# The last convolution of a graph network: edge rows loaded two steps ahead, a ring of eight, and another order of PE's and ACT's work in a step

## The chip, the cores and the metric

The kernel runs on one core of a Trainium2 chip. The metric is the device time of one execution in microseconds (us), lower is better. The median of three runs of the kernel before is 12377.51 us.

## The reference

Four message-passing layers of a graph network run one after the other on 6250 nodes and 100000 edges; after each, `x = layernorm(x + layer(x))`. The change touches the edge part of the last layer alone. Cut to that part:

```python
h = silu(edge_scalars @ fcW1 * (1.0 / sqrt(8)))          # (E, 8) @ (8, 64)
w = h @ fcW2 * (1.0 / sqrt(64))                          # (E, 64) @ (64, 192)
wA, wB, wC, wD = w[:, :64], w[:, 64:128], w[:, 128:160], w[:, 160:192]
xs, xv = f_s[edge_src], f_v[edge_src]                    # gather: 64 scalars, 32 vectors of 3
y0, y1 = edge_attr[:, :1], edge_attr[:, 1:4]
outA = wA * xs * y0
outD = wD * einsum('eud,ed->eu', xv, y1) / sqrt(3)
outB = wB[:, :, None] * xs[:, :, None] * y1[:, None, :]
outC = wC[:, :, None] * xv * y0[:, :, None]
edge_feat = concatenate([outA, outD, outB, outC])        # 384 numbers an edge
agg = segment_sum(edge_feat, edge_dst, num_segments=n)   # edges are sorted by edge_dst
```

All of it is float32. `tab_src` in the kernel holds f_s and f_v of each node (160 numbers).

## The kernel before, in words

`plain_convolution` (lines 1718 to 1881) does this part. Edges are taken in macro tiles of 4 x 128 (TM = 4 edges on each of 128 partitions). The loop has V = 244 entries, which the text below calls edge steps or indices: 196 macro tiles and 48 more passes over tiles that straddle a block of target nodes. A table `W["block"]` says which tile an index reads.

For an index i the work runs in stages on five queues, each stage one or more steps after the one before it. An engine's program is a list of steps; in step n it does, in the order in which the code has them, each of its stages for index n minus the stage's number (TURN 0, PRE 1, WEIGHTS 2, PRODUCT 3, SUM 4, TOTAL 5, STORE 6). The engines are held together only by semaphores.

- SP loads the edge rows `er` (128 x 64 floats, line 1751) and stores `total` (line 1755). The load for index i waits until `products` of index i - 4 are done, because `er` has four buffers. Its block number comes from memory by a `value_load`.
- POOL waits for `er`, issues 4 indirect DMAs that gather 128 node rows each into `g` (line 1772), and adds a shift to the target numbers, `rel` (line 1775). `g` and `rel` also have four buffers.
- PE (TensorE) turns the edge rows (TURN, `psE`, line 1789), multiplies them by the first map (PRE, `psH`, line 1803), the result by the second (WEIGHTS, `psW`, line 1810), and sums the products by a one-hot matrix (SUM, `psS`, line 1796). In the profile one float32 matmul is two records.
- ACT copies the turned rows (`esT`, line 1822), applies silu (`h`, line 1827), and scales the gathered rows (`feat_y`, `g0` in the code, four instructions, line 1833).
- DVE makes the products in `rows` (lines 1853 to 1868, the last one signals `products`), the one-hot matrix `hot` (line 1870), and adds `psS` to a running `total` (line 1877).

`steps` writes the first and last steps out and loops over the rest, RING steps to a turn of the loop. `psE` and `psH` have one buffer; `psW`, `psS`, `rows`, `hot`, `esT`, `h` and `g0` have two.

Of the kernel before, what the change touches and what calls it, by code (L numbers as in the profile page):

```python
# [16 lines left out]
I32 = mybir.dt.int32  # L17
ALU = mybir.AluOpType
ACT = mybir.ActivationFunctionType
AX = mybir.AxisListType  # L20

P = 128
N_NODES, N_EDGES = 6250, 100000
C0, C1 = 64, 32
C1V = 3 * C1
CX = C0 + C1V
# [5 lines left out]
TM = 4  # L32
# [6 lines left out]
V = NM + BOUNDS  # L39
ER = 16  # L40
# [4 lines left out]
class Names:  # L45
# [17 lines left out]
    def sem(self, name):  # L63
        if name not in self.sems:
            self.sems[name] = self.nc.alloc_semaphore(f"{self.tag}_{name}")
        return self.sems[name]


def wait(eng, sem, value):

    if not isinstance(value, int) or value > 0:
        eng.wait_ge(sem, value)


def wait_apart(eng, sem, value, passed):

    if not isinstance(value, int):
        eng.wait_ge(sem, value)
        eng.sem_inc(passed, 1)
    elif value > 0:  # L80
        eng.wait_ge(sem, value)
# [41 lines left out]
def bcast(ap, axis, n):  # L123

    ap = ap.unsqueeze(axis)
    shape = list(ap.shape)
    shape[axis] = n
    return ap.to_broadcast(shape)
# [456 lines left out]
def comp(ap, n=3):  # L585

    return ap.rearrange("p t (d c) -> p t d c", d=n)
# [1130 lines left out]
def plain_convolution(nc, W, D, tag):  # L1718

    TURN, PRE, WEIGHTS, PRODUCT, SUM, TOTAL, STORE = 0, 1, 2, 3, 4, 5, 6
    LAST, RING = STORE, 4
    width = SUM_W[3]
    sums = D["sums"][3]
    with ExitStack() as ctx:
        S = Names(nc, ctx, tag)
        sem = S.sem
        ring = lambda name, shape, n, dt=F32: [S.sb(f"{name}{u}", shape, dt) for u in range(n)]
        er, g = ring("er", [P, TM, ER], RING), ring("g", [P, TM, CX], RING)  # L1730
        rel, hot = ring("rel", [P, TM], RING, I32), ring("hot", [P, TM, P], 2)
        esT, h = ring("esT", [ER * TM, P], 2), ring("h", [64, ME], 2)
        g0, prod, dot, bs = ring("feat_y0", [P, TM, CX], 2), S.sb("prod", [P, TM, C1V]), S.sb("dot", [P, TM, C1]), S.sb("bs", [P, TM, C0])
        rows, total = ring("rows", [P, TM, width], 2), ring("total", [P, width], RING)
        psE, psH = S.ps("psE", [ER * TM, 512]), S.ps("psH", [64, 512])
        psWs = [S.ps(f"psW{u}", [P, TM, 256]) for u in range(2)]
        psS = [S.ps(f"psS{u}", [P, 512]) for u in range(2)]
# [3 lines left out]
        @block.sync  # L1741
        def _(sp):
            sp.dma_start(sums[0], W["zeros"][:, 0:width]).then_inc(sem("first"), 16)

            def body(i_of):
                if m := i_of(0):
                    i, u, j = m
                    wait_apart(sp, sem("products"), i - RING + 1, sem("sp_passed"))
                    wait_apart(sp, sem("rel"), i - RING + 1, sem("sp_passed"))
                    at = sp.value_load(W["block"][0:1, bass.ds(i, 1)], min_val=0, max_val=NM - 1)  # L1750
                    sp.dma_start(er[u][:, :, :].rearrange("p t c -> p (t c)"), block_at(edges, at)).then_inc(sem(f"er{u}"), 16)
                if m := i_of(STORE):
                    i, u, j = m
                    wait_apart(sp, sem("totals"), i + 1, sem("sp_passed"))
                    sp.dma_start(sums[bass.ds(i + 1, 1), :, :].rearrange("o p c -> (o p) c"), total[u][:, :]).then_inc(sem(f"stored{u}"), 16)

            steps(sp, V, LAST, body, RING)
            sp.wait_ge(sem("first"), 16)
            for u in range(RING):
                sp.wait_ge(sem(f"stored{u}"), 16 * (V // RING))  # L1760

        @block.gpsimd
        def _(pool):
            passed = sem("pool_passed")

            def body(i_of):
                if m := i_of(0):
                    i, u, j = m
                    wait_apart(pool, sem(f"er{u}"), (j + 1) * 16, passed)
                    wait_apart(pool, sem("products"), i - RING + 1, passed)  # L1770
                    for k in range(TM):
                        pool.indirect_dma_start(g[u][:, k, :], None, D["tab_src"], bass.IndirectOffsetOnAxis(er[u][:, k, 12:13].bitcast(I32), 0))\  # L1772
                            .then_inc(sem(f"gathered{u}"), 16)
                    wait_apart(pool, sem("hot"), i - RING + 1, passed)
                    nc.gpsimd.tensor_tensor(rel[u][:, :], er[u][:, :, 13].bitcast(I32), W["shift"][:, bass.ds(i, 1)].to_broadcast([P, TM]), ALU.add)\
                        .then_inc(sem("rel"), 1)

            steps(pool, V, LAST, body, RING)

        @block.tensor  # L1780
        def _(pe):
            passed = sem("pe_passed")

            def body(i_of):
                if m := i_of(TURN):
                    i, u, j = m
                    wait_apart(pe, sem(f"er{u}"), (j + 1) * 16, passed)
                    wait_apart(pe, sem("esT"), i, passed)
                    nc.tensor.transpose(psE[:, 0:P], er[u][:, :, :].rearrange("p t c -> p (t c)"), W["ident"][:, :]).then_inc(sem("es_T"), 1)
                if m := i_of(SUM):  # L1790
                    i, u, j = m
                    wait_apart(pe, sem("hot"), i + 1, passed)
                    wait_apart(pe, sem("products"), i + 1, passed)
                    wait_apart(pe, sem("totals"), i - 1, passed)
                    for k in range(TM):
                        last = nc.tensor.matmul(psS[u % 2][:, 0:width], hot[u % 2][:, k, :], rows[u % 2][:, k, :], start=(k == 0), stop=(k == TM - 1))  # L1796
                    last.then_inc(sem("summed"), 1)
                if m := i_of(PRE):
                    i, u, j = m
                    wait_apart(pe, sem("esT"), i + 1, passed)  # L1800
                    wait_apart(pe, sem("h"), i, passed)
                    for k in range(TM):
                        last = nc.tensor.matmul(psH[:, P * k:P * k + P], W["l3_fc1"][:, 64 * k:64 * k + 64], esT[u % 2][:, :], start=True, stop=True)
                    last.then_inc(sem("pre"), 1)
                if m := i_of(WEIGHTS):
                    i, u, j = m
                    wait_apart(pe, sem("h"), i + 1, passed)
                    wait_apart(pe, sem("products"), i - 1, passed)
                    for k in range(TM):
                        last = nc.tensor.matmul(psWs[u % 2][:, k, 0:192], h[u % 2][:, P * k:P * k + P], W["l3_fc2"][:, :], start=True, stop=True)  # L1810
                    last.then_inc(sem("weights"), 1)

            steps(pe, V, LAST, body, RING)

        @block.scalar
        def _(act):
            def body(i_of):
                if m := i_of(TURN):
                    i, u, j = m
                    act.wait_ge(sem("es_T"), i + 1)  # L1820
                    wait(act, sem("pre"), i - 1)
                    nc.scalar.activation(esT[u % 2][:, :], psE[:, 0:P], ACT.Copy).then_inc(sem("esT"), 1)
                if m := i_of(PRE):
                    i, u, j = m
                    act.wait_ge(sem("pre"), i + 1)
                    wait(act, sem("weights"), i - 1)
                    nc.scalar.activation(h[u % 2][:, :], psH[:, :], ACT.Silu, scale=1.0 / float(np.sqrt(8.0))).then_inc(sem("h"), 1)
                if m := i_of(WEIGHTS):
                    i, u, j = m
                    act.wait_ge(sem(f"gathered{u}"), (j + 1) * 16 * TM)  # L1830
                    wait(act, sem("products"), i - 1)
                    for k in range(TM):
                        last = nc.scalar.activation(g0[u % 2][:, k, :], g[u][:, k, :], ACT.Copy, scale=er[u][:, k, 8:9])
                    last.then_inc(sem("g0"), 1)

            steps(act, V, LAST, body, RING)

        @block.vector
        def _(dve):
            tt = nc.vector.tensor_tensor  # L1840
            nc.vector.memset(total[RING - 1][:, :], 0.0).then_inc(sem("empty"), 1)

            def body(i_of):
                if m := i_of(PRODUCT):
                    i, u, j = m
                    psW, R = psWs[u % 2], rows[u % 2]
                    s, v = g[u][:, :, 0:C0], comp(g[u][:, :, C0:CX])
                    s0, v0 = g0[u % 2][:, :, 0:C0], comp(g0[u % 2][:, :, C0:CX])
                    D3 = R[:, :, 96:width].rearrange("p t (d c) -> p t d c", d=3)
                    Y = bcast(er[u][:, :, 9:12], 3, C1)  # L1850
# [16 lines left out]
                    dve.wait_ge(sem("dot"), i + 1)  # L1867
                    tt(R[:, :, C0:96], psW[:, :, 160:192], dot[:, :, :], ALU.mult).then_inc(sem("products"), 1)
                    dve.wait_ge(sem("rel"), i + 1)
                    tt(hot[u % 2][:, :, :], bcast(W["lane"][:, :], 1, TM), bcast(rel[u][:, :], 2, P), ALU.is_equal).then_inc(sem("hot"), 1)  # L1870
                if m := i_of(TOTAL):
                    i, u, j = m
                    dve.wait_ge(sem("summed"), i + 1)
# [935 lines left out]
```

## Time and profile before

| | |
|---|---|
| median of 3 runs | 12377.51 us |
| lowest and highest run | 12340.81 and 12393.03 us |
| span of the profiled execution | 13633.7 us |
| this part, first to last start of its SUM matmuls | 11404.8 to 13286.7 us |

No time of the profiled execution other than its span is at hand. The span is 10% above the median of the runs, so a difference of durations in the trace is one of the profiled execution.

The page divides the span in 40 slices; this part lies in the slices 34 to 39. The views used below are the waits (who waited for whom), the groups of instructions, the timeline (instructions in order of time, with the idle time before each and who ended it), and the busy time of each engine in stretches, with the granted clock of TensorE as a share of full speed (1.00 is 2.4 GHz, 0.50 is 1.2 GHz).

### The profile page before, as it was taken

Reading aid. Unit: us, or ns where it says so; the run is one execution under the profiler, and the core shown is the slowest. Engines: PE = TensorE matmul, PEld = TensorE weight load, DVE = VectorE, ACT = ScalarE, POOL = GpSimd, SP = SyncE. Lnnn points to the kernel's source line nnn. Section 1 sums busy time; section 2 is a strip of 40 time slices with the busy share of each in tenths; the row PEclk is TensorE's granted clock in tenths of the full one; section 3 lists DMA queues with packets and bytes.
Section 4 is the critical chain, followed back from the end, with each engine's and each line's share of the span. In section 5 each row is a group of like instructions: output and inputs, shape, how many; then the busy total and the mean of one; then the engine's idle time right before and its main releaser. Section 6 shows DMA issues by size and latency. Waiting matters only on the chain. (4 is left out here: it accounts for less than half of the span.)

```text
span 13633.7 us, 220854 instructions
## 1 busy us (share of the span) xinstructions
PE 9563.9 (70%) x44805; PEld 7451.6 (55%) x44805; DVE 8593.3 (63%) x21214; ACT 4334.4 (32%) x10856; POOL 8081.0 (59%) x8212
## 2 busy tenths in 40 slices
PE   2998989863656666666655777777775657888885
PEld 2888888853544222222244666666664545555554
DVE  4677777778734555555534777777777765555553
ACT  1444444430022222222212555555554002222221
POOL 4777777755624888888822555555552643555550
PEclk7777777777956777777765888888887987888885
DMA  3444444435602888888852222222221652222221
GB/s 93 105 107 103 107 102 107 105 100 158 188 20 50 132 132 132 131 132 131 132 148 85 68 69 68 68 69 69 68 69 49 183 134 57 71 71 70 73 72 46
DMA packets 1350634, 1320.06 MB, mean 97 GB/s; under 512 B 508622, under 2 KB 1147330, under 8 KB 1349894
## 3 DMA queue, kind: packets, MB, share of 16 engines
q0 software_dynamic: 347904, 594.12, 23.6%
q1 hardware_dynamic: 854716, 713.61, 18.2%
q10 hardware_dynamic: 147914, 11.21, 0.8%
q8 instruction: 37, 0.61, 0.0%
q14 instruction: 63, 0.52, 0.0%
HBM read 800.64 MB, written 517.55 MB: 97 GB/s over the span
## 5 line engine op out<-in xcount | busy, mean ns | idle before, releaser
L737 POOL DMA_INDIRECT e_gs<-tab_src,e_ix x1568 | 1685.9, 1075 | 1253.8 <-DVE e_msg L2066 785.5
L737 POOL DMA_INDIRECT e_gd<-tab_dst,e_ix x1568 | 1670.5, 1065 | 478.0 <-issue 473.4
L676 PE MATMUL e_psF<-w_ident,e_F 128*128 128x128 f32 x6272 | 1394.2, 335 | 727.6 <-ACT e_F L1954 495.6
L788 PE MATMUL e_psS<-e_rows,e_same 128*128 128x480 f32 x1568 | 1113.4, 876 | 857.7 <-DVE e_same L762 857.7
L1772 POOL DMA_INDIRECT e_g<-tab_src,e_er x976 | 977.0, 1001 | 852.0 <-DMA e_er<-edge_rows 600.8
L676 PEld LDWEIGHTS e_psF<-w_ident,e_F 128*128 128x128 f32 x6272 | 951.5, 180 | 895.9 <-issue 844.5
L806 POOL DMA_INDIRECT acc<-e_sums,e_row x784 | 1248.6, 1593 | 239.0 <-issue 220.5
L706 ACT ACTIVATE e_FT<-e_psF 128x384 f32<-128x384 f32 (+1 forms) x2352 | 1069.7, 455 | 941.7 <-PE e_psF L676 587.3
L788 PEld LDWEIGHTS e_psS<-e_rows,e_same 128*128 128x128 f32 x1568 | 431.4, 293 | 1549.4 <-issue 1522.2
L1563 PE MATMUL s_psS<-s_wv,s_hot 128*128 128x168 f32 (+1 forms) x3904 | 714.2, 331 | 596.0 <-POOL s_wv L1521 574.8
L712 ACT ACTIVATE e_O<-e_psO 128x352 f32<-128x352 f32 (+1 forms) x1568 | 689.7, 440 | 995.6 <-remote 434.0
L1563 PEld LDWEIGHTS s_psS<-s_wv,s_hot 128*128 128x128 f32 x3904 | 606.7, 203 | 703.1 <-issue 490.4
L737 POOL DMA_INDIRECT e_g<-tab_src,e_ix x784 | 822.8, 1050 | 248.6 <-issue 183.2
L796 ACT ACTIVATE e_sums<-e_psS 128x480 f32<-128x480 f32 x784 | 447.8, 571 | 1513.7 <-issue 1089.8
L1796 PE MATMUL e_psS<-e_rows,e_hot 128*128 128x384 f32 x1952 | 914.7, 626 | 20.1 <-issue 14.6
L2266 POOL TENSOR_TENSOR n_st<-n_st,w_half 128x8 f32<-128x8 f32 x70 | 113.5, 1638 | 1085.4 <-DVE n_st L2691 937.1
L1684 DVE TENSOR_TENSOR e_prod<-e_g,e_dirs 128x384 f32<-128x384 f32 x196 | 109.4, 558 | 887.8 <-DMA e_g<-tab_src,e_ix 837.4
L1796 PEld LDWEIGHTS e_psS<-e_rows,e_hot 128*128 128x128 f32 x1952 | 459.1, 247 | 345.3 <-issue 230.2
L1485 POOL TENSOR_TENSOR s_wv<-s_val,s_pb 128x128 f32<-128x128 f32 x976 | 614.5, 649 | 0.0
L1855 DVE TENSOR_TENSOR e_bs<-e_psW,e_g 128x256 f32<-128x256 f32 x244 | 102.8, 421 | 785.5 <-remote 457.2
L686 PE MATMUL e_psO<-w_l_t,e_FT 128*128 128x160 f32 x1568 | 471.9, 394 | 98.2 <-ACT e_O L712 85.7
L2384 ACT ACTIVATE n_sT<-n_psA 64x512 f32<-64x512 f32 x70 | 41.4, 591 | 1441.0 <-PE n_psA L2280 1439.4
(492 smaller groups left out, 25450.2 us busy)
## 6 DMA issues: line engine op xcount, KB each, us to landing
s_val<-val SPq DMA_DIRECT2D x488, 320.0 KB
val<-e_O SPq DMA_DIRECT2D x392, 320.0 KB
acc<-w_zeros SPq DMA_DIRECT2D x392, 139.5 KB
n_ag<-acc SPq DMA_DIRECT2D x56, 960.0 KB
e_krow<-in_src_t SPq DMA_DIRECT2D x196, 256.0 KB
sums<-e_total SPq DMA_DIRECT2D x244, 192.0 KB
e_es<-in_es SPq DMA_DIRECT2D x196, 130.0 KB
e_gs<-tab_src,e_ix POOLq DMA_INDIRECT x1568
```

Of the source, the lines that this page charges most:

```text
L676: last = nc.tensor.transpose(psF[:, P * g:P * g + P], F[:, k, P * g:P * g + P], ident[:, :])
L686: nc.tensor.matmul(o[:, 0:first], f[:, 0:P], W[w + "_t0"][:, :], start=True, stop=True, skip_group_check=True)
L706: nc.scalar.activation(FT[:, k, :], psF[:, 0:width], ACT.Copy).then_inc(S.sem(tag + "_FT"), 1)
L712: nc.scalar.activation(O[:, k, :], o[:, 0:width], ACT.Copy).then_inc(S.sem(tag + "_O"), 1)
L737: pool.indirect_dma_start(into[t][u][:, k, :], None, tables[t], bass.IndirectOffsetOnAxis(ix[u][:, t, k:k + 1], 0))\
L788: nc.tensor.matmul(psS[(k) % len(psS)], T["same"][u][:, k, :], values[:, k, :], start=True, stop=True)\
L796: nc.scalar.activation(T["sums"][u][:, k, :], psS[k % len(psS)], ACT.Copy).then_inc(S.sem("sums"), 1)
L806: pool.indirect_dma_start(acc[k], bass.IndirectOffsetOnAxis(T["row"][u][:, k:k + 1], 0), T["sums"][u][:, k, :], None, compute_op=ALU.add). ...
L1485: return tt(heads(wv), heads(val), bcast(pb[u][:, :, :], 3, n // H), ALU.mult)
L1563: last = nc.tensor.matmul(psS[u][:, 0:width], hot[u][:, k, :], wv[u][:, k, :], start=(k == 0), stop=(k == TM - 1))
L1772: pool.indirect_dma_start(g[u][:, k, :], None, D["tab_src"], bass.IndirectOffsetOnAxis(er[u][:, k, 12:13].bitcast(I32), 0))\
L1796: last = nc.tensor.matmul(psS[u % 2][:, 0:width], hot[u % 2][:, k, :], rows[u % 2][:, k, :], start=(k == 0), stop=(k == TM - 1))
```

## The change

The stages get other numbers: the load of `er` stays at 0, gather, `rel` and TURN move from 0 to 2, and all others move by 2 as well. So seen from the gather, the load comes two steps earlier and nothing else moves by a whole step. `er`, `total` and their semaphores get eight buffers; `g` and `rel` keep four (ROWS4). The load for index i now waits for `products` of index i - 8. A turn of the loop holds eight steps in place of four.

Inside a step PE does TURN, PRE, WEIGHTS, SUM in place of TURN, SUM, PRE, WEIGHTS. ACT does `feat_y`, `esT`, `h` in place of `esT`, `h`, `feat_y`.

```diff
-    TURN, PRE, WEIGHTS, PRODUCT, SUM, TOTAL, STORE = 0, 1, 2, 3, 4, 5, 6
-    LAST, RING = STORE, 4
+    GATHER, PRE, WEIGHTS, PRODUCT, SUM, TOTAL, STORE = 2, 3, 4, 5, 6, 7, 8
+    TURN, LAST, RING, ROWS4 = GATHER, STORE, 8, 4
...
-        er, g = ring("er", [P, TM, ER], RING), ring("g", [P, TM, CX], RING)
-        rel, hot = ring("rel", [P, TM], RING, I32), ring("hot", [P, TM, P], 2)
+        er, g = ring("er", [P, TM, ER], RING), ring("g", [P, TM, CX], ROWS4)
+        rel, hot = ring("rel", [P, TM], ROWS4, I32), ring("hot", [P, TM, P], 2)
...
-                if m := i_of(0):
+                if m := i_of(GATHER):
                     i, u, j = m
                     wait_apart(pool, sem(f"er{u}"), (j + 1) * 16, passed)
-                    wait_apart(pool, sem("products"), i - RING + 1, passed)
+                    wait_apart(pool, sem("products"), i - ROWS4 + 1, passed)
...
-                    wait_apart(pool, sem("hot"), i - RING + 1, passed)
+                    wait_apart(pool, sem("hot"), i - ROWS4 + 1, passed)
...
@@ PE: the blocks PRE and WEIGHTS now stand ahead of SUM
+                if m := i_of(PRE):
...
+                if m := i_of(WEIGHTS):
...
                 if m := i_of(SUM):
...
-                if m := i_of(PRE):
...
-                if m := i_of(WEIGHTS):
...
@@ ACT: the block WEIGHTS (feat_y) now stands ahead of TURN and PRE
+                if m := i_of(WEIGHTS):
...
                 if m := i_of(TURN):
...
-                if m := i_of(WEIGHTS):
...
```

On PE, at the head of the loop of this part, one step before reads as follows (`L78` and `L106` are registers and the loop).

```order
L106 ISA
L78 REGISTER_ALU
L1789 MATMUL e_psE<-w_ident,e_er 64x128
L78 ISA
L78 REGISTER_ALU
L1796 MATMUL e_psS<-e_rows,e_hot 128x384 x4
L78 REGISTER_ALU x2
L1803 MATMUL e_psH<-e_esT,w_l_fc 64x128 x4
L1810 MATMUL e_psW<-w_l_fc,e_h 128x192 x4
```

The same place of the changed kernel, where PRE has line 1795, WEIGHTS 1802 and SUM 1810:

```order
L106 ISA
L78 ISA
L1789 MATMUL e_psE<-w_ident,e_er 64x128
L78 REGISTER_ALU
L1795 MATMUL e_psH<-e_esT,w_l_fc 64x128 x4
L78 REGISTER_ALU
L1802 MATMUL e_psW<-w_l_fc,e_h 128x192 x4
L78 REGISTER_ALU
L1810 MATMUL e_psS<-e_rows,e_hot 128x384 x4
```

The sum of 4 matmuls has moved behind the two maps; no matmul was added or taken away.

On ACT, in the second step of the loop, the order before was:

```order
L1822 ACTIVATE e_esT<-e_psE 64x128
L1827 ACTIVATE e_h<-e_psH 64x512
L1833 ACTIVATE e_feat_y<-e_g,e_er 128x160 x4
```

And now, with `feat_y` at line 1823, `esT` at 1829 and `h` at 1834:

```order
L1823 ACTIVATE e_feat_y<-e_g,e_er 128x160 x4
L1827 REGISTER_ALU
L1829 ACTIVATE e_esT<-e_psE 64x128
L1834 ACTIVATE e_h<-e_psH 64x512
```

The four scalings of gathered rows now stand first, so whatever they wait for holds the copy of the turned rows too.

## Rows read from the trace of the kernel before

**Rows 1.** Windows: busy us (count) of each engine, granted clock, DMA share.

```profile
core 0: us, PE busy (x) PEld busy (x) DVE busy (x) ACT busy (x) POOL busy (x), PEclk, DMA share, GB/s
11400.00:13290.00 1890.00, 1579.99 (x6072) 992.68 (x6071) 1081.43 (x2438) 514.94 (x1455) 1031.26 (x1212) 0.83 0.27 72
```

**Rows 2.** Waits, 11420 to 13250 us: who waited for whom, total us, times, longest.

```profile
POOL e_g L1772 <- DMA e_er<-edge_rows: 577.6, 135, 9.2
...
DVE e_bs L1855 <- remote: 449.4, 61, 11.7
...
PE e_psE L1789 <- DMA e_er<-edge_rows: 274.7, 118, 5.2
```

**Rows 3.** Timeline of PE: start, us, what, idle time before it.

```profile
12302.54 0.30 PE L1789 MATMUL e_psE<-w_ident,e_er 128*64 128x128 f32 x1
12302.68 2.75 PE L1796 MATMUL e_psS<-e_rows,e_hot 128*128 128x384 f32 x8
12305.35 1.08 PE L1803 MATMUL e_psH<-e_esT,w_l_fc 64*64 64x128 f32 x8
12306.37 1.56 PE L1810 MATMUL e_psW<-w_l_fc,e_h 64*128 64x192 f32 x8
12309.95 0.39 PE L1789 MATMUL e_psE<-w_ident,e_er 128*64 128x128 f32 x1 [2.02 <-DMA e_er<-edge_rows]
12310.41 5.46 PE L1796 MATMUL e_psS<-e_rows,e_hot 128*128 128x384 f32 x8
...
12318.31 0.30 PE L1789 MATMUL e_psE<-w_ident,e_er 128*64 128x128 f32 x1
```

**Rows 4.** Timeline of DVE, SP's queue and POOL: the load behind that wait.

```profile
12305.85 0.28 DVE L1868 TENSOR_TENSOR e_rows<-e_psW,e_dot 128x128 f32<-128x128 f32 x1
...
12307.73 0.34 SPq L1751 DMA_DIRECT2D e_er<-edge_rows  x1
...
12310.47 0.97 POOL L1772 DMA_INDIRECT e_g<-tab_src,e_er  x1 [3.70 <-DMA e_er<-edge_rows]
```

**Rows 5.** Windows around that wait.

```profile
12308.00:12309.00 1.00, 0.00 (x0) 0.00 (x0) 0.89 (x2) 1.00 (x4) 0.00 (x0) 0.98 0.14 31
...
12310.00:12312.00 2.00, 1.94 (x4) 1.07 (x5) 2.00 (x6) 0.27 (x1) 1.22 (x2) 0.50 0.00 0
```

**Rows 6.** Timeline of POOL: one step that waited for no load.

```profile
12301.14 0.20 POOL L1775 TENSOR_TENSOR e_rel<-e_er,w_shift 128x4 int32<-128x4 int32 x1
12301.50 0.97 POOL L1772 DMA_INDIRECT e_g<-tab_src,e_er  x1 [0.15 <-issue]
...
12304.02 0.95 POOL L1772 DMA_INDIRECT e_g<-tab_src,e_er  x1 [0.30 <-issue]
...
12306.29 0.48 POOL L1775 TENSOR_TENSOR e_rel<-e_er,w_shift 128x4 int32<-128x4 int32 x1
```

**Rows 7.** Sources: count, ns min/median/max of one, first and last start.

```profile
L1772 POOL DMA_INDIRECT e_g<-tab_src,e_er x976: 942/949/1542, 11390.7 to 13267.4; - x196
...
L1866 DVE TENSOR_TENSOR e_rows<-e_bs,e_er x488: 539/547/615, 11401.1 to 13282.6; 128x384 f32<-128x384 f32 x163
...
L1796 PE MATMUL e_psS<-e_rows,e_hot x1952: 486/486/980, 11404.9 to 13287.0; 128*128 128x384 f32 x196
```

**Rows 8.** Groups and a window of the first layer: its gathers, its engines' load.

```profile
L737 POOL DMA_INDIRECT e_gs<-tab_src,e_ix x1568 | 1685.9, 1075 | 1253.8 <-DVE e_msg L2066 785.5
500.00:2400.00 1900.00, 1703.19 (x9368) 1564.84 (x9366) 1372.42 (x3412) 870.34 (x1842) 1461.24 (x1288) 0.75 0.43 106
```

**Rows 9.** Timeline of DVE: one index, to the next `prod`.

```profile
12319.11 0.42 DVE L1855 TENSOR_TENSOR e_bs<-e_psW,e_g 128x256 f32<-128x256 f32 x1 [5.78 <-PE e_psW L1810]
...
12319.95 0.41 DVE L1861 TENSOR_TENSOR e_rows<-e_psW,e_feat_y 128x256 f32<-128x256 f32 x1
...
12321.88 0.68 DVE L1870 TENSOR_TENSOR e_hot<-w_lane,e_rel 128x512 f32<-128x512 int32 x1
...
12323.00 0.55 DVE L1853 TENSOR_TENSOR e_prod<-e_g,e_er 128x384 f32<-128x384 f32 x1
```

More of the change, by code:

```diff
@@ L1759, in _ @@
             for u in range(RING):
-                sp.wait_ge(sem(f"stored{u}"), 16 * (V // RING))
+                sp.wait_ge(sem(f"stored{u}"), 16 * -(-(V - u) // RING))
         @block.gpsimd
@@ L1766, in body @@
             def body(i_of):
-                if m := i_of(0):
+                if m := i_of(GATHER):
                     i, u, j = m
                     wait_apart(pool, sem(f"er{u}"), (j + 1) * 16, passed)
-                    wait_apart(pool, sem("products"), i - RING + 1, passed)
+                    wait_apart(pool, sem("products"), i - ROWS4 + 1, passed)
                     for k in range(TM):
-                        pool.indirect_dma_start(g[u][:, k, :], None, D["tab_src"], bass.IndirectOffsetOnAxis(er[u][:, k, 12:13].bitcast(I32), 0))\
+                        pool.indirect_dma_start(g[u % ROWS4][:, k, :], None, D["tab_src"], bass.IndirectOffsetOnAxis(er[u][:, k, 12:13].bitcast(I32), 0))\
                             .then_inc(sem(f"gathered{u}"), 16)
-                    wait_apart(pool, sem("hot"), i - RING + 1, passed)
-                    nc.gpsimd.tensor_tensor(rel[u][:, :], er[u][:, :, 13].bitcast(I32), W["shift"][:, bass.ds(i, 1)].to_broadcast([P, TM]), ALU.add)\
+                    wait_apart(pool, sem("hot"), i - ROWS4 + 1, passed)
+                    nc.gpsimd.tensor_tensor(rel[u % ROWS4][:, :], er[u][:, :, 13].bitcast(I32), W["shift"][:, bass.ds(i, 1)].to_broadcast([P, TM]), ALU.add)\
                         .then_inc(sem("rel"), 1)
@@ L1789, in body @@
                     nc.tensor.transpose(psE[:, 0:P], er[u][:, :, :].rearrange("p t c -> p (t c)"), W["ident"][:, :]).then_inc(sem("es_T"), 1)
[L1790 to L1797, printed above, removed]
                 if m := i_of(PRE):
@@ L1811, in body @@
                     last.then_inc(sem("weights"), 1)
+                if m := i_of(SUM):
+                    i, u, j = m
+                    wait_apart(pe, sem("hot"), i + 1, passed)
+                    wait_apart(pe, sem("products"), i + 1, passed)
+                    wait_apart(pe, sem("totals"), i - 1, passed)
+                    for k in range(TM):
+                        last = nc.tensor.matmul(psS[u % 2][:, 0:width], hot[u % 2][:, k, :], rows[u % 2][:, k, :], start=(k == 0), stop=(k == TM - 1))
+                    last.then_inc(sem("summed"), 1)
             steps(pe, V, LAST, body, RING)
@@ L1817, in body @@
             def body(i_of):
+                if m := i_of(WEIGHTS):
+                    i, u, j = m
+                    act.wait_ge(sem(f"gathered{u}"), (j + 1) * 16 * TM)
+                    wait(act, sem("products"), i - 1)
+                    for k in range(TM):
+                        last = nc.scalar.activation(g0[u % 2][:, k, :], g[u % ROWS4][:, k, :], ACT.Copy, scale=er[u][:, k, 8:9])
+                    last.then_inc(sem("g0"), 1)
                 if m := i_of(TURN):
@@ L1827, in body @@
                     nc.scalar.activation(h[u % 2][:, :], psH[:, :], ACT.Silu, scale=1.0 / float(np.sqrt(8.0))).then_inc(sem("h"), 1)
-                if m := i_of(WEIGHTS):
[L1829 to L1834, printed above, removed]
             steps(act, V, LAST, body, RING)
@@ L1846, in body @@
                     psW, R = psWs[u % 2], rows[u % 2]
-                    s, v = g[u][:, :, 0:C0], comp(g[u][:, :, C0:CX])
+                    s, v = g[u % ROWS4][:, :, 0:C0], comp(g[u % ROWS4][:, :, C0:CX])
                     s0, v0 = g0[u % 2][:, :, 0:C0], comp(g0[u % 2][:, :, C0:CX])
@@ L1869, in body @@
                     dve.wait_ge(sem("rel"), i + 1)
-                    tt(hot[u % 2][:, :, :], bcast(W["lane"][:, :], 1, TM), bcast(rel[u][:, :], 2, P), ALU.is_equal).then_inc(sem("hot"), 1)
+                    tt(hot[u % 2][:, :, :], bcast(W["lane"][:, :], 1, TM), bcast(rel[u % ROWS4][:, :], 2, P), ALU.is_equal).then_inc(sem("hot"), 1)
                 if m := i_of(TOTAL):
```

## The prediction

> **What bounds the kernel now.** The kernel is a chain of parts, so only the last convolution counts. Its SUM matmuls start from 11404.9 to 13287.0 us [rows 7]; for 244 indices that is 243 intervals, 1882.1 us, 7.745 us each. The windows show no engine full: PE 84% (1579.99 of 1890 us), DVE 57%, POOL 55%, DMA 27%, at a granted clock of 0.83 [rows 1]. So something waits in rings, and the waits say for what: POOL waited 577.6 us and PE 274.7 us for one thing, the load of the edge rows [rows 2]. Two thirds of DVE's waits (449.4 us) have no releaser on record; its product waits for weights that PE makes, so I count them as PE's lateness.
>
> The timeline of PE shows the rhythm, in pairs. An undisturbed step is SUM, PRE, WEIGHTS and a turn: from 12302.54 to 12307.93, less an overlap of 0.06 as there is between PRE and WEIGHTS: 5.33 us, PE's floor. Then PE stands 2.02 us for the load, and its next SUM takes 5.46 us in place of 2.75; two steps took 12318.31 - 12302.54 = 15.77 us [rows 3]. Why the load is late: the last product of an index ends at 12306.13, SP issues the load 1.6 us later at 12307.73, and gather and turn can start at 12310.47 and 12309.95, 3.8 us after the product at best [rows 4]. The load waits for the product four indices back, and the turn that needs it is first in PE's step: the ring is one load too short. The slow SUM is the clock: it was still 0.98 in the first us of the idle time, and it was 0.50 from 12310 on, although PE was busy again [rows 5]. PE's idle time is thus paid twice.
>
> The interval splits as 5.33 (floor) + 1.16 (274.7 us over the 236 steps of that stretch [rows 2]) + 1.26 left, which I put down to the half clock: 2.71 us more for one SUM in each pair would be 1.35.
>
> **The change, part by part.** All terms are us of an interval, in the profiled execution.
>
> *The load, two steps ahead, eight buffers.* It is issued after the product eight indices back. The gather of index m may not start before products of m - 4 (`g` still has four buffers), and the load of m needs only those of m - 8, which is four intervals, over 20 us, earlier; SP does it behind a store that waits for a total of an older index. Against 3.8 us of latency this leaves slack of many us. Removed: 1.16 on PE, and POOL's 577.6 us of waits. With PE no longer idle, the 1.26 of half clock should go as well. Lower bound if only these count: 5.33. If this cover failed (SP kept back by its store), the old 3.8 us would be back in every step.
>
> *PE's order.* The same matmuls. PRE now follows TURN, but reads the copy made one step earlier; WEIGHTS reads silu of the step before, and one whole SUM (2.75 us) lies between. New: PE's last work of a step is SUM, and DVE writes `rows` over those that SUM two indices back has read. DVE can start with `bs` and `dot` after WEIGHTS, but must then wait for SUM's end, that is for the end of PE's step. From the first write of `rows` to the end of `hot` it needs 12322.56 - 12319.95 = 2.61 us; the whole index, from `bs` to the end of the next `prod`, takes 12323.55 - 12319.11 = 4.44 [rows 9]. The next SUM that needs these rows comes a full PE step and two maps later, about 8 us. Cost 0; hidden by PE's own step. Behind DVE's wait stand `hot` and `total`, for which PE waits only one step later, so the same slack covers them.
>
> *ACT's order.* `feat_y` needs gathers two steps old and products of m - 4, which end about 3 us before the step in which its copy is wanted; ACT's own work is 514.94 us over 244 indices, 2.1 us [rows 1]. Cost 0; without that cover a late gather would hold `esT`, and through it PE's next turn.
>
> *Longer loop.* Eight steps a turn, 28 turns for 58, two steps more to fill and drain in which only a load or a store runs: under 2 us together, not counted.
>
> *What is late next.* DVE needs 4.44, PE 5.33. POOL: an unhindered step is 12306.29 - 12301.14 = 5.15 us: `rel`, 0.15, and four gathers of 0.95 to 0.97 with 0.30 between them [rows 6]. That is nearly PE's floor, and it will not stay unhindered: gathers here take 949 ns in the median and up to 1542 [rows 7]. So far POOL had its busy times when DVE often stood still. The nearest row with a denser DVE is the first layer's: DVE 1372.42 of 1900 us, 72%, gathers of 1075 ns in the mean [rows 8]. DVE will be about 80% busy (4.44 of 5.6). Four gathers of 1.075, three gaps of 0.30, `rel` at 0.25 (0.20 and 0.48 in rows 6) and 0.15 behind it make 5.60. Bounds: 5.15 from below, and from above all gathers and `rel` at the longest seen, 4 x 1.542 + 0.90 + 0.48 + 0.15 = 7.70. I take 5.60, since the first layer's mean is the nearest row; POOL then sets the pace, not PE, and PE idles 0.27 us a step, too little by rows 5 to think that the clock falls.
>
> **A rule weighed.** DVE's products of two operands in SBUF (line 1866) took 539 to 615 ns, whatever POOL did [rows 7]; gathers, on the other hand, went up to 1542. The Trainium skill, "SBUF — State Buffer", section "SBUF: two separate sides", says that a DVE instruction with two SBUF inputs and a GpSimd one that reads SBUF exclude each other for their whole length. By this rule no gather would run beside lines 1853, 1866 or 1870. The trace agrees by half: the gather pays, DVE never does by more than 0.07 us. What full exclusion would give is a rival below.
>
> **The sum.** 7.745 - 5.60 = 2.145 us, times 243 is 521 us of the span of 13633.7. The runs' median is 9.2% under that span, and nothing shows which waits shrink without the profiler. If all shrink alike, the gain is 521 x 0.908 = 473; if this part doesn't shrink, 521. The middle is 497, a factor of 0.954: 12377.5 - 497 = 11880 us.
>
> **Rivals.**
> 1. *The part is worth less unprofiled* (0.18). If the interval before shrinks by 9.2% to 7.03 while matmul and gather times stay, the gain is 1.43 x 243 = 347: 12030 us. If the load's latency shrinks more than the mean, less still, to about 12150. For it: load latency and SP's 1.6 us are waits, the stuff that a profiler stretches. Against: half of the loss sits in matmuls at half clock.
> 2. *POOL and DVE exclude each other* (0.10). Then a step of POOL is its busy time, 4 x 0.949 + 0.208, plus DVE's `prod`, two of line 1866 and `hot`, 0.55 + 1.09 + 0.68 [rows 7, 9]: 6.32 us; gain 1.42 x 243 x 0.954 = 330: 12047 us. For it: the maxima of the gathers. Against: in rows 6 the gather at 12304.02 took 0.95 with DVE at work.
> 3. *No change* (0.06): another ring takes over the wait at once, at about 7.7 us. The candidate is `g` with four buffers: gather (5.15), landing (taken as the load's 2.2 us, 12309.95 less 12307.73), `feat_y` and product (about 2 and 4.4) around four indices, 13.8 / 4 = 3.4 us a step. It does not reach 5.33, so I give it little.
> 4. *Slower* (0.05): the clock stays at half though PE works. A PE step is then twice the floor, 10.66 us, and the gain turns into a loss of 2.915 x 243 x 0.954 = 676 us: 13053. It decides from the point where 45% of the steps run so, (7.745 - 5.33) / 5.33. For it: in the first layer PE is 90% busy and the granted clock is 0.75 [rows 8]; with half of the time at half clock the step would be 5.33 / 0.75 = 7.11, still faster, at 12230. Against: rows 3 and 5, where a fully busy PE brought the clock back within one step.
> 5. *Better than my case* (0.03): POOL at 5.15 and PE at 5.33, unshrunk, 2.415 x 243 = 587: 11790 us.
>
> **How the numbers follow.** My forecast, an interval of 5.3 to 5.9, has 0.58. It covers about 11790 to 12000. A measurement of this kernel tells about 0.5% from no change (62 us). The range runs from 11790, case 5, to 12100, which takes in rival 2 and most of rival 1: 0.58 + 0.10 + 0.13, about 0.8. Faster by over 0.5% are the forecast and rivals 1, 2 and 5, 0.89, less a little for the smallest of rival 1: 0.88. Within 0.5%: 0.07. Slower: 0.05.
>
> **What would show it.** In the changed kernel's profile: the waits of PE and POOL for `er` gone; SUM matmuls 1360 us from first to last; granted clock above 0.95 in the part; POOL nearly without waits, gathers near 1075 ns; DVE waiting for `summed` each step, less than 1 us. Wrong would be: PE waiting for ACT's copy at its turn (a late gather), a clock near 0.8 with SUM matmuls of 980 ns, gathers above 1.2 us in the mean, or the interval after falling in the trace and not in the runs.

## The result and the profile after

| | before | changed |
|---|---|---|
| median of 4 timed runs, us | 12382.14 | 12152.06 |
| lowest and highest run, us | 12340.81, 12393.03 | 12142.17, 12165.48 |
| this part, first to last SUM, profiled | 1882.1 [rows 7] | 1309.8 |
| one interval (243 of them), profiled | 7.745 | 5.39 |

The ratio is 0.983, 95% interval 0.9814 to 0.9847. The change makes the kernel faster, by 230 us, less than half of the 497 forecast; the time lies above the range. The traces show a larger difference, 572 us in this part alone, but the two profiled executions are not alike: that of the kernel before has a span of 13633.7 us, 10% above its timed runs, that of the changed kernel 12140.4, and that execution took 12142.17 us. What the first trace shows is told under the experiments.

The changed kernel's windows over all of this part and inside it (columns as in [rows 1]):

```profile
10480.00:11800.00 1320.00, 1315.61 (x6060) 891.36 (x6059) 1081.99 (x2431) 542.63 (x1452) 1040.84 (x1208) 1.00 0.38 102
10600.00:11700.00 1100.00, 1100.00 (x5097) 746.12 (x5096) 907.54 (x2040) 457.81 (x1224) 879.14 (x1021) 1.00 0.39 103
```

From 10600 to 11700 us PE is busy all the time, at full granted clock. Its waits from 10600 to 11700 us, and the sources that answer to [rows 7]:

```profile
ACT e_esT L1829 <- PE e_psE L1789: 296.4, 204, 1.6
ACT e_feat_y L1823 <- DMA e_g<-tab_src,e_er: 196.4, 204, 1.1
DVE e_rows L1861 <- PE e_psS L1810: 192.5, 204, 0.9
POOL e_g L1772 <- issue: 188.7, 626, 0.3
```

```profile
L1810 PE MATMUL e_psS<-e_rows,e_hot x1952: 486/486/1007, 10486.2 to 11796.0; 128*128 128x384 f32 x196
...
L1772 POOL DMA_INDIRECT e_g<-tab_src,e_er x976: 942/946/1121, 10467.1 to 11780.8; - x196
```

No engine waits for `er` in this stretch, against 577.6 and 274.7 us in [rows 2]. ACT waits in each step for the gathered rows (196.4 us in 204 waits), which costs nothing here, because PE doesn't wait for ACT. The timeline, PE and one instruction of DVE, shows a step of 5.39 us without a hole, from turn to turn:

```profile
11200.54 2.85 PE L1810 MATMUL e_psS<-e_rows,e_hot 128*128 128x384 f32 x8
11203.23 0.27 PE L1789 MATMUL e_psE<-w_ident,e_er 128*64 128x128 f32 x1
11203.43 0.42 DVE L1861 TENSOR_TENSOR e_rows<-e_psW,e_feat_y 128x256 f32<-128x256 f32 x1 [0.94 <-PE e_psS L1810]
11203.43 1.08 PE L1795 MATMUL e_psH<-e_esT,w_l_fc 64*64 64x128 f32 x8
11204.44 1.56 PE L1802 MATMUL e_psW<-w_l_fc,e_h 64*128 64x192 f32 x8
...
11208.62 0.27 PE L1789 MATMUL e_psE<-w_ident,e_er 128*64 128x128 f32 x1
```

DVE now waits 0.94 us for the end of SUM before it may write `rows`, as forecast.

### The profile page after: what moved, and what is told of

The parts are those of the page before. It is cut to its first block and busy times, and to the rows that moved or that the text cites. A ratio compares the mean times of both kernels' runs of the same rounds, so it can differ in the third digit from the quotient of the medians.

```text
span 12140.4 us, 219938 instructions
## 1 busy us (share of the span) xinstructions
PE 8894.9 (73%) x44805; PEld 7005.1 (58%) x44805; DVE 8560.0 (71%) x21214; ACT 4341.0 (36%) x10856; POOL 8069.6 (66%) x8212
## 5 line engine op out<-in xcount | busy, mean ns | idle before, releaser
L737 POOL DMA_INDIRECT e_gd<-tab_dst,e_ix x1568 | 1732.2, 1105 | 477.8 <-issue 477.5
L737 POOL DMA_INDIRECT e_gs<-tab_src,e_ix x1568 | 1640.0, 1046 | 501.3 <-issue 436.3
L676 PE MATMUL e_psF<-w_ident,e_F 128*128 128x128 f32 x6272 | 1264.6, 310 | 245.3 <-ACT e_F L1954 232.7
L676 PEld LDWEIGHTS e_psF<-w_ident,e_F 128*128 128x128 f32 x6272 | 876.1, 166 | 377.6 <-issue 336.4
L1810 PE MATMUL e_psS<-e_rows,e_hot 128*128 128x384 f32 x1952 | 696.7, 500 | 0.8 <-DVE e_total L1877 0.8
L1010 DVE TENSOR_TENSOR e_hn<-e_raw,e_rstd 128x256 f32<-128x256 f32 x398 | 151.4, 422 | 509.5 <-POOL e_rstd L884 509.5
L1810 PEld LDWEIGHTS e_psS<-e_rows,e_hot 128*128 128x128 f32 x1952 | 351.9, 190 | 251.3 <-issue 56.4
L983 PE MATMUL e_psW<-w_l_rw,e_h 65*128 65x224 f32 x1568 | 393.5, 401 | 139.4 <-DVE e_F L1072 134.6
```

Of the source, the lines that this page charges most:

```text
L676: last = nc.tensor.transpose(psF[:, P * g:P * g + P], F[:, k, P * g:P * g + P], ident[:, :])
L737: pool.indirect_dma_start(into[t][u][:, k, :], None, tables[t], bass.IndirectOffsetOnAxis(ix[u][:, t, k:k + 1], 0))\
L983: last = nc.tensor.matmul(psW[:, k, 0:224], h2[v][:, P * k:P * k + P], W["l0_rw3"][:, :], start=True, stop=True)
```

## The experiments

Two questions: why the gain was 230 us and not 497, and which part of the change makes it. On the first, theory A says that the trace shown before had more waits than the timed runs; its rival says that the interval really was 7.7 us and that the gain was lost elsewhere. On the second, the forecast had put everything on the loads and nothing on the order. All times are medians; "before" is the kernel before on the same chip. The chips differ: the kernel before takes about 12350 us on some, called ordinary below, and about 14060 on others, called slow chips, so only times of one chip are compared.

### The kernel before again, and this part twice

The first run is the kernel before, unchanged. The second calls this part a second time, with buffers of its own and the same output:

```diff
                 plain_convolution(nc, W, D, "e3")
+                plain_convolution(nc, W, D, "f3")
```

> The kernel before, unchanged, profiled once more. Theory A (the trace of before was taken in a slow execution, and the runs that are timed are faster in this part too): the span comes out near the timed 12382 us, not 13634, and the SUM matmuls of the last convolution take about 1540 us from first to last, 6.3 us an interval, since the change left 1310 us and gained 230; POOL's and PE's waits for the edge rows are well under the 577.6 and 274.7 us shown. Rival B (the profiler stretches this kernel each time, and not the changed one): the span is again near 13630 us and the interval near 7.7 us, while the time measured stays at 12382.

> The kernel before with its last convolution run twice in a row, which leaves the output as it is. The added time is what the part costs without any help of a profile. Theory A: 1540 us more than before, about 13920 us in all. Rival B': the part does cost 1880 us in timed runs, and the change loses 340 us elsewhere: 1880 us more, about 14260.

Measured: 12348.27 us, ratio 1.0003 (0.9988 to 1.0018), and 13905.45 against 12350.51, ratio 1.1262 (1.1221 to 1.1304), so a second call costs 1555 us. Theory A had forecast 1540, its rival 1880. Sources, waits (10700 to 11800 us) and window of the kernel before, again:

```profile
L1796 PE MATMUL e_psS<-e_rows,e_hot x1952: 486/486/980, 10472.6 to 11983.8; 128*128 128x384 f32 x196
```

```profile
DVE e_bs L1855 <- PE e_psW L1810: 297.1, 176, 4.1
...
POOL e_g L1772 <- DMA e_er<-edge_rows: 119.5, 74, 3.0
...
PE e_psE L1789 <- DMA e_er<-edge_rows: 41.6, 71, 0.9
```

```profile
10700.00:11800.00 1100.00, 1024.92 (x4487) 669.62 (x4486) 796.53 (x1791) 373.49 (x1074) 757.63 (x896) 0.97 0.34 91
```

The interval is 1511.2 / 243 = 6.22 us, and the added call takes 1555 unprofiled against 1882.1 in the first trace: theory A holds, its rival falls. PE waits for the same loads, but 0.23 us a step (41.6 us over 179.5 steps) in place of 1.16, and no wait is put down to "remote", the name that the view gives to a wait whose releaser it doesn't find. The span is 12331.6 and this execution took 12333.45 us, beside a median of 12348.27: here the profile did not stretch the execution.

The spans of this trace and of the changed kernel's differ by 191.2 us, their parts by 201.4: on ordinary executions trace and runs agree.

### Loads alone, order alone

Loads alone is the changed kernel with the blocks of PE and ACT back in their old order; order alone is the kernel before with the two orders of the changed one. Shown for PE:

```diff
@@ loads alone, against the changed kernel
+                if m := i_of(SUM):
...
                 if m := i_of(PRE):
...
-                if m := i_of(SUM):
...
@@ order alone, against the kernel before
-                if m := i_of(SUM):
...
                 if m := i_of(PRE):
...
+                if m := i_of(SUM):
...
```

> The changed kernel with PE's and ACT's order of before: loads two steps ahead, ring of eight. Theory A says that the loads are the whole change: 12152 us, as the changed kernel, interval 5.4 us, granted clock 1.00. Rival C (the order does part of it, since SUM then no longer stands between a turn and the first map): slower than the changed kernel by over 0.5%, 12215 us or more.

> The kernel before with PE's and ACT's new order alone; loads, stage numbers and rings as before. Theory A: within 0.5% of before, 12320 to 12445 us, the waits for edge rows unchanged. Rival C: over 0.5% faster than before. Third: slower than before by over 0.5%, since the turn that waits for the edge rows now holds both maps back directly, with no SUM between.

Measured, on the chip of the last two: loads alone 12120.42, ratio 0.9809 (0.9777 to 0.9841), interval (11773.4 - 10478.5) / 243 = 5.33; order alone 12143.77, ratio 0.9831 (0.98 to 0.9862), interval (11803.1 - 10481.1) / 243 = 5.44. The first came out as theory A has it, rival C fell: the new order is not needed for the gain. But the second was a miss for theory A: order alone, which the forecast held to be worth nothing, brings nearly as much as the whole change. Its sources and its window:

```profile
L1810 PE MATMUL e_psS<-e_rows,e_hot x1952: 485/486/1007, 10481.1 to 11803.1; 128*128 128x384 f32 x196
```

```profile
10600.00:11700.00 1100.00, 1093.33 (x5050) 739.30 (x5049) 898.80 (x2020) 452.30 (x1210) 880.04 (x1009) 1.00 0.39 102
```

### Which of the two orders

> The kernel before with PE's new order alone (SUM last in a step), rings and loads as before. Theory E (the order alone gained 207 us because DVE does its first two products during SUM, so that the last product, and with it the load of the edge rows, comes 0.9 us earlier after PE's last step): as the kernel with both orders, about 12145 us. Rival F (ACT's order did it: feat_y no longer stands behind silu): no gain, 12350.

> The kernel before with ACT's new order alone (feat_y first). Theory E: no gain, 12310 to 12400 us. Rival F: about 12145.

The edits are the halves of the last one, PE's blocks alone and ACT's alone. Measured against 12349.75: PE's order 12162.91, ratio 0.984 (0.9817 to 0.9862), interval (11807.1 - 10485.9) / 243 = 5.44; ACT's 12346.21, ratio 0.9987 (0.9974 to 0.9999), interval (12000.0 - 10475.6) / 243 = 6.27. All but 4 us of it is PE's order. One of the four runs with PE's order took 19345.35 us, the other three 12156.51 to 12165.2; why is not known, and without it the median would be 12160.62. The mechanism stands in the timelines, of DVE, SP's queue and PE. First the kernel before, again:

```profile
11202.93 1.56 PE L1810 MATMUL e_psW<-w_l_fc,e_h 64*128 64x192 f32 x8
...
11204.53 0.42 DVE L1855 TENSOR_TENSOR e_bs<-e_psW,e_g 128x256 f32<-128x256 f32 x1 [0.87 <-PE e_psW L1810]
...
11207.10 0.28 DVE L1868 TENSOR_TENSOR e_rows<-e_psW,e_dot 128x128 f32<-128x128 f32 x1
...
11208.35 0.34 SPq L1751 DMA_DIRECT2D e_er<-edge_rows  x1
...
11214.83 0.34 SPq L1751 DMA_DIRECT2D e_er<-edge_rows  x1
...
11216.91 0.27 PE L1789 MATMUL e_psE<-w_ident,e_er 128*64 128x128 f32 x1 [0.51 <-DMA e_er<-edge_rows]
```

PE's step ends with WEIGHTS, at 11204.49. DVE begins with `bs` 0.04 later and its last product ends at 11207.38; the load goes out 0.97 later, and 2.08 us after a load (11214.83 to 11216.91) a turn that waited for it can start. Together 0.04 + 2.85 + 0.97 + 2.08 = 5.94 us from the end of one step to the turn of the next but one, and between the two lies one step of 5.33: by this sum the turn waits 0.61, then the step after has no wait, and so in pairs. The waits shown by this trace at three turns in a row are 0.60, none and 0.51. Such a wait often costs more than itself:

```profile
10655.86 0.27 PE L1789 MATMUL e_psE<-w_ident,e_er 128*64 128x128 f32 x1 [0.55 <-DMA e_er<-edge_rows]
10656.52 4.51 PE L1796 MATMUL e_psS<-e_rows,e_hot 128*128 128x384 f32 x8 [0.39 <-issue]
```

Of the 206 SUMs from 10600 to 11900 us 31 took over 4 us. Now order alone:

```profile
11205.32 0.27 PE L1789 MATMUL e_psE<-w_ident,e_er 128*64 128x128 f32 x1
...
11205.52 0.42 DVE L1861 TENSOR_TENSOR e_rows<-e_psW,e_feat_y 128x256 f32<-128x256 f32 x1 [1.29 <-PE e_psS L1810]
...
11207.26 0.28 DVE L1868 TENSOR_TENSOR e_rows<-e_psW,e_dot 128x128 f32<-128x128 f32 x1
...
11208.50 0.33 SPq L1751 DMA_DIRECT2D e_er<-edge_rows  x1
...
11210.76 0.27 PE L1789 MATMUL e_psE<-w_ident,e_er 128*64 128x128 f32 x1
```

SUM is last here, from 11202.63 on, so DVE has done `bs` (from 11203.31) and `dot` (from 11203.64) under it and needs only the writes of `rows` after it. The load goes out 3.18 us after the next turn began, that is after the end of SUM; with 2.08 from load to turn that is 5.26, under PE's own 5.39. The wait goes because the loop got shorter, without another buffer.

### Load one step ahead

This is the changed kernel with eight buffers, gather one step behind the load:

```diff
-    GATHER, PRE, WEIGHTS, PRODUCT, SUM, TOTAL, STORE = 2, 3, 4, 5, 6, 7, 8
+    GATHER, PRE, WEIGHTS, PRODUCT, SUM, TOTAL, STORE = 1, 2, 3, 4, 5, 6, 7
```

> The changed kernel with the load one step ahead of the gather in place of two, ring of eight. The load then has one more interval, 5.4 us, against about 3.2 us of latency. Theory A: the same as the changed kernel, 12140 to 12165 us, no waits for edge rows. Rival (two steps are needed): waits for edge rows return, over 12200 us.

It was run with the changed kernel, loads alone and the changed kernel with this part called twice, on a chip where the kernel before takes 14068.76 us.

> The changed kernel once more, in five rounds, beside the version with early loads and the old order. Known so far: 12152 us, interval 5.39 us. Expected: 12140 to 12165.

> Early loads with the old order of PE and ACT, in five rounds on the same chip as the changed kernel. The trace of the first run had 5.33 us an interval against 5.39 with the new order, 15 us in all. Theory D (the new order costs a seam on PE, once the loads are early): 12115 to 12140 us, at least 10 us under the changed kernel. Rival: the two are equal, and the 12120 of the first run was the chip.

> The changed kernel with its last convolution run twice. Adds the part's cost with no profile: 1330 us (1310 for the SUM matmuls and 20 to fill and drain, as the kernel before twice added 1555 for 1540), so about 13480 us. The difference of the two doublings, 1555 less 1330, is then the gain of about 225 us. If the added time is above 1400, part of the gain is lost outside of the part.

Measured: one step ahead 13730.56, ratio 0.9757 (0.9724 to 0.9789); changed 13718.99, 0.9759 (0.9733 to 0.9786); loads alone 13738.92, 0.9765 (0.9738 to 0.9792); called twice 15420.62, 1.0969 (1.0933 to 1.1004), 1702 us over the changed kernel. One step ahead is as good as two on this chip; on an ordinary one it was not run. The expectations in absolute times were for an ordinary chip. That of loads alone, at least 10 us under the changed kernel, was missed: it was 20 us over. The limit of 1400 us for the second call can't be applied either, since the part takes 13369.2 - 11707.9 = 1661.3 us here, and the kernel before was not called twice on this chip. Here PE is not always busy in the changed kernel; its waits and its window from 11800 to 12800 us:

```profile
ACT e_esT L1829 <- remote: 320.3, 46, 8.9
...
POOL e_g L1772 <- DVE e_rows L1868: 213.6, 50, 5.3
...
DVE e_bs L1855 <- remote: 124.7, 25, 8.7
```

```profile
11800.00:12800.00 1000.00, 894.72 (x3635) 589.87 (x3634) 642.69 (x1453) 305.30 (x872) 630.87 (x725) 0.90 0.30 81
```

"remote" is back, and it is also in the trace on which the forecast rests [rows 2].

### A later load, before and after

SP reads the block number from memory three times in place of once ahead of each load, in the kernel before and in the changed one:

```diff
                     at = sp.value_load(W["block"][0:1, bass.ds(i, 1)], min_val=0, max_val=NM - 1)
+                    at = sp.value_load(W["block"][0:1, bass.ds(i, 1)], min_val=0, max_val=NM - 1)
+                    at = sp.value_load(W["block"][0:1, bass.ds(i, 1)], min_val=0, max_val=NM - 1)
```

> The kernel before with the block number read three times in place of once before each load of edge rows, which delays the load by an estimated 1.0 to 1.4 us (a whole product end to load issue takes 0.97 us with one read). Theory A (in the kernel before the load's latency lies on the chain product, load, turn, weights, product, once an interval): the whole delay is added to each interval, 240 to 340 us, to 12590 to 12690 us. Rival G (SP's work is hidden and the interval is set elsewhere): under 60 us more.

> The changed kernel with the same two further reads before each load. Theory A: nothing, since the load is issued over 15 us before it is needed, and SP has 5.39 us for about 4: within 0.5% of 12152. Rival: SP becomes the bound or holds the stores back, and over 60 us are added.

Measured: before with it 12650.02, ratio 1.0232 (1.0214 to 1.0251), interval (12303.1 - 10487.7) / 243 = 7.47; changed with it 12135.95, ratio 0.9822 (0.9804 to 0.984), interval 5.39. The kernel before got 300 us slower, within the 240 to 340 forecast, the changed one did not: its load has time to spare. Waits from 10700 to 12100 us, the window and the timeline of PE, DVE and SP's queue of the kernel before with the late load (lines are 2 further down):

```profile
POOL e_g L1774 <- DMA e_er<-edge_rows: 415.8, 97, 5.8
...
PE e_psE L1791 <- DMA e_er<-edge_rows: 167.1, 93, 2.1
```

```profile
10700.00:12100.00 1400.00, 1212.25 (x4657) 761.62 (x4656) 827.68 (x1860) 387.48 (x1118) 784.21 (x931) 0.84 0.27 74
```

```profile
11196.49 2.75 PE L1798 MATMUL e_psS<-e_rows,e_hot 128*128 128x384 f32 x8
...
11203.58 0.39 PE L1791 MATMUL e_psE<-w_ident,e_er 128*64 128x128 f32 x1 [1.84 <-DMA e_er<-edge_rows]
11204.24 5.46 PE L1798 MATMUL e_psS<-e_rows,e_hot 128*128 128x384 f32 x8 [0.27 <-issue]
...
11204.35 0.28 DVE L1870 TENSOR_TENSOR e_rows<-e_psW,e_dot 128x128 f32<-128x128 f32 x1
...
11206.71 0.34 SPq L1753 DMA_DIRECT2D e_er<-edge_rows  x1
```

This is the picture of [rows 3] on an ordinary chip: pairs, 1.84 us of idle time, a SUM of 5.46 (granted clock 0.50 from 11204 to 11210). A later load alone makes such waits, and the long matmuls come with them. From the last product (end 11204.63) to the load (11206.71) it is now 2.08 us for 0.97.

### Before, changed and loads alone on one chip

> The kernel before once more. Theory A: the interval depends on the chip, not on the kernel. If the kernel before runs here in about 12350 us, its trace has no late signals and an interval of 6.2 to 6.4 us. If it runs above 13000 us, its trace shows the shown one's pattern: waits of DVE put down to a remote signal, hundreds of us, and an interval above 7.5. The rival (it was the profiler): an interval near 7.7 in a trace whose runs stay at 12350.

> The changed kernel, for comparison with loads alone on one chip. Theory D (the new order of PE costs 0.06 us in each of 243 intervals once loads are early): loads alone is 15 us faster than this one, 0.1%. The rival (both the same): no difference beyond the scatter of some 10 us. On a slow chip neither will show.

> Early loads with the old order of PE and ACT. Theory D: an interval of 5.33 and a time 15 to 30 us under the changed kernel's of this call. The rival: 5.39 and the same time.

Measured, against a before of 14058.71: before 14061.22, ratio 1.0003 (0.9986 to 1.002); changed 13712.4, 0.9755 (0.9728 to 0.9782); loads alone 13728.71, 0.9764 (0.9736 to 0.9792). Loads alone and the changed kernel are not told apart here: loads alone is 16 us slower, where theory D expected 15 to 30 less. The kernel before on this chip, waits from 11720 to 13700 us, window, and DVE's timeline at the end of a WEIGHTS:

```profile
DVE e_bs L1855 <- remote: 864.4, 106, 9.4
POOL e_g L1772 <- DMA e_er<-edge_rows: 736.4, 121, 7.9
...
PE e_psE L1789 <- DMA e_er<-edge_rows: 380.6, 117, 6.4
```

```profile
11900.00:13500.00 1600.00, 1275.39 (x4737) 790.87 (x4736) 837.22 (x1900) 403.18 (x1138) 799.60 (x949) 0.80 0.24 66
```

```profile
12303.76 1.56 PE L1810 MATMUL e_psW<-w_l_fc,e_h 64*128 64x192 f32 x8
...
12307.59 0.42 DVE L1855 TENSOR_TENSOR e_bs<-e_psW,e_g 128x256 f32<-128x256 f32 x1 [7.84 <-remote]
```

WEIGHTS ends at 12305.32 and `bs` starts 2.27 us later, where it was 0.04 on the ordinary chip; the product and the load behind it are late with it. That is the first trace's pattern, stronger: "remote" 864.4 us for 449.4, and an interval of (13710.1 - 11675.7) / 243 = 8.37. All ten runs took over 14040 us, so it is this chip, for as long as it was measured, and not one execution. That it is not this part alone is seen in the second layer's attention, which the change doesn't touch. The same source in the first trace, in the kernel before again, and on this chip:

```profile
L2066 DVE TENSOR_TENSOR e_msg<-e_gs,e_gd x196: 811/818/827, 7427.8 to 10408.6; 128x640 f32<-128x640 f32 x196
```

```profile
L2066 DVE TENSOR_TENSOR e_msg<-e_gs,e_gd x196: 808/818/867, 7238.9 to 9473.3; 128x640 f32<-128x640 f32 x196
```

```profile
L2066 DVE TENSOR_TENSOR e_msg<-e_gs,e_gd x196: 815/818/841, 7506.1 to 10669.2; 128x640 f32<-128x640 f32 x196
```

One instruction takes 818 ns on all three, but its loop takes 2981, 2234 and 3163 us. On which chip the first trace was taken is not on record; its span of 13633.7 us lies between the two kinds.

## Why the prediction was wrong

A step has 25 records of matmuls, so a window's count gives its steps, and its busy time splits them (us for one step; the first row from [rows 1], the others from the inner windows above):

| kernel | steps | step | PE busy | PE idle | clock |
|---|---|---|---|---|---|
| before, trace shown | 242.9 | 7.78 | 6.50 | 1.28 | 0.83 |
| before, again | 179.5 | 6.13 | 5.71 | 0.42 | 0.97 |
| before, late load | 186.3 | 7.52 | 6.51 | 1.01 | 0.84 |
| before, slow chip | 189.5 | 8.44 | 6.73 | 1.71 | 0.80 |
| changed | 203.9 | 5.39 | 5.39 | 0 | 1.00 |
| changed, slow chip | 145.4 | 6.88 | 6.15 | 0.72 | 0.90 |

**The step that failed** is the base of the sum, at two places of the prediction. "Two thirds of DVE's waits (449.4 us) have no releaser on record; [...] so I count them as PE's lateness": in part `bs` started late though PE had finished. (It is 449.4 of the 763.2 us that `bs` waited, 59%; the rest is 230.3 on PE and 83.5 with no releaser shown either.) Even the shown rows have it: the step's WEIGHTS ended before the turn at 12318.31 [rows 3], `bs` came at 12319.11 [rows 9]. And "nothing shows which waits shrink without the profiler. If all shrink alike ...": the profiler stretches nothing, see the kernel before again. The 10% between the span and the runs belonged to one execution with waits that the others don't have, and they don't lie evenly: this part is 25% longer (1882.1 for 1511.2), the second layer's attention 33% (2981 for 2234). So 7.745 us stood for 6.22, which is 1.525 x 243 x 0.954 = 353 us of forecast gain. That these waits make the interval longer is shown by the slow chip and by the late load; what makes them is open. Against it the interval after was better by 0.21 (49 us), and the factor 0.954 took 9 us off the real 202 (0.83 x 243). 497 - 353 + 49 + 9 = 202 us, beside 230 between the medians and 189 to 230 by the ratio's interval. Rival 1 came nearest, down to 12150 us, with the right place and the wrong reason: not the profiler, but the execution.

**The loads.** Right: all waits for `er` are gone, in the changed kernel and in loads alone, also with the load 1.1 us later. On an ordinary chip the step before had 0.42 us of idle time, of which 0.23 for the loads, and 0.38 of matmuls slower than the floor of 5.33, not 1.16 and 1.26.

**PE's order, "Cost 0".** Wrong in what it left out: the sum asked only what the order costs, and not that it brings the load forward. It has a cost and a worth. Alone it shortens the way from PE's step to the load by 5.94 - 5.26 = 0.68 us and so gives 187 us, or 207 together with ACT's. Both parts remove the same wait, so they don't add: 187 us for PE's order (12349.75 - 12162.91), 230 for the loads (12350.51 - 12120.42), 230 for both together. Once the loads are early, the order lengthens the step on an ordinary chip from 5.33 to 5.39, SUM 2.85 in the timeline for 2.75. That is 0.06 x 243 = 15 us by the traces; the times don't confirm it, and on the slow chips the kernel with the order was 20 and 16 us the faster one, within the scatter.

**ACT's order, "Cost 0".** Right, ratio 0.9987 alone.

**POOL sets the pace at 5.60.** Wrong by size: gathers of 1.075 us were expected, and they took 987 ns in the mean with DVE busy 907.54 of 1100 us. The first line is the changed kernel's, the second that of loads alone, both from 10600 to 11700 us:

```profile
L1772 POOL DMA_INDIRECT e_g<-tab_src,e_er x817 | 806.3, 987 | 217.4 <-issue 188.7
```

```profile
L1772 POOL DMA_INDIRECT e_g<-tab_src,e_er x828 | 834.3, 1008 | 220.7 <-issue 220.7
```

POOL's busy time and its gaps are 879.14 + 217.4 = 1096.5 us for 203.9 steps, 5.38 each, against 5.39 of PE: POOL has no spare time that the trace shows, and its term was nearly right. That PE sets the pace is argued: with its old order it takes 5.32 us a step (1100 us over 206.9 steps), within 0.01 of the floor from [rows 3], and POOL then does its step in 5.30.

Rival 2, full exclusion of POOL and DVE, would be 6.32 us. The Trainium skill, "SBUF — State Buffer", section "SBUF: two separate sides", has such an exclusion between a DVE instruction with two SBUF inputs and a GpSimd one that reads SBUF. For these gathers the trace does not agree: the step is 5.39, the longest gather 1121 ns, and the one below took its 0.95 us although `prod` ran beside it.

```profile
11201.00 0.95 POOL L1772 DMA_INDIRECT e_g<-tab_src,e_er  x1 [0.30 <-issue]
11201.10 0.55 DVE L1853 TENSOR_TENSOR e_prod<-e_g,e_er 128x384 f32<-128x384 f32 x1
```

**The clock.** Right: 1.00 in the changed kernel's part, and the half clock of [rows 5] went with the wait.

**On a slow chip** the change gives more, 346 us (14058.71 - 13712.4), though PE still stands idle 0.72 us a step there. Nothing in the sum foresaw the 6.88 us that it settles at: waits without a known releaser are then found elsewhere, such as before `esT`.

## What to carry to other kernels

Put the profile's span beside the timed runs first; where it is 10% longer and large waits have no releaser, as here, the interval of the trace is not that of the runs. Profile once more, or call the part twice and time that. A wait for a load in a ring of buffers is a loop: write down every link from the step's end to the next use. Shortening any link, such as what the engine does last in its step, can do the same as another buffer, and two cures of one wait do not add. Early loads alone do what the whole change does (12120.42 us, ratio 0.9809 beside 0.983), so the new order is not needed; which of the two is better the runs don't decide.

## What the runs showed of the hardware

- Two kinds of chips: the same kernel took 12348.27 us on one and 14061.22 on another, with equal instruction times (818 ns, above). The difference is in the idle times between instructions, for example `bs` 0.04 or 2.27 us after WEIGHTS. Whether the signal or the instruction came late there, and why, stays open.
- Idle time on PE of 1.84 us was followed by a SUM at half clock, 5.46 for 2.75 us. Shorter waits did it at times: one of 0.55 us, with 0.39 more before SUM, was followed by a SUM of 4.51, one of 0.60 (at 11205.09 in the same trace) was not. The mean granted clock was 0.97 there.
- Two more reads of a register from memory on SP moved the load by 1.11 us, 0.55 each.
- A load of edge rows took 2.08 us from its issue to the start of the turn that waited for it.
